# mLSTM heads: the mask of the first diagonal block moved to GpSimd, in place, ahead of a batch's finishing steps

## What is computed

```
log_fg = where(lower triangle, cum[s] - cum[t], -inf)
log_D  = log_fg + ig[t]
max_log_D = max(log_D, axis=-1)
D  = exp(log_D - max_log_D)
C  = (q k^T / sqrt(32)) * D
Cn = C / (max(|sum C|, exp(-max_log_D)) + 1e-6)
h  = Cn v
mu = mean(h);  var = mean((h - mu)^2)
out = (h - mu) * rsqrt(var + 1e-6) * ln_scale
x   = x + out
```

## Time and profile before

| what | value |
|---|---|
| median of three runs | 1442.99 us (1439.77 to 1443.45) |
| profiled execution, its own time | 1437.92 us |
| its span (first to last instruction) | 1436.1 us |
| mean granted TensorE clock | 0.896 |
| busy: PE / DVE / ACT / POOL | 78% / 61% / 35% / 32% |
| head stage, from the first load's landing to the last GpSimd instruction | 512.8 to 710.1 us |

### The profile page before, as it was taken

The page is one execution under the profiler, slowest core; times in us unless marked ns, Lnnn a source line. Parts: engine busy times, 40 slices in busy tenths (PEclk is TensorE's granted clock), DMA queues, the critical chain, the costliest instruction groups (busy, mean ns, idle before and its releaser), DMA issues. The chain is left out here.

```text
span 1436.1 us, 22899 instructions
## 1 busy us (share of the span) xinstructions
PE 1126.7 (78%) x6304; PEld 855.0 (60%) x6322; DVE 870.6 (61%) x1590; ACT 495.8 (35%) x1051; POOL 455.5 (32%) x344
## 2 busy tenths in 40 slices
PE   7998898788848468898178881559999999999942
PEld 6988665344425258787166650447777776777730
DVE  3344478788746348877254438945767767666515
ACT  2231252666622256775021110013333333333310
POOL 0000011111000005866722210125566656566520
PEclk9999899999989769887679995869999999999985
DMA  6210500000016495660131007058789988877639
GB/s 238 72 66 3 187 1 1 1 0 0 1 35 224 144 264 160 188 190 1 52 123 39 29 15 249 0 175 183 201 189 232 239 205 232 200 193 187 119 48 362
DMA packets 117608, 181.20 MB, mean 126 GB/s; under 512 B 13401, under 2 KB 48729, under 8 KB 117568
## 3 DMA queue, kind: packets, MB, share of 16 engines
q1 hardware_dynamic: 97184, 137.40, 29.6%
q0 software_dynamic: 18080, 38.85, 13.9%
q10 hardware_dynamic: 2304, 4.46, 0.8%
HBM read 138.76 MB, written 46.93 MB: 129 GB/s over the span
## 5 line engine op out<-in xcount | busy, mean ns | idle before, releaser
L2001 POOL DMA_INDIRECT y_d<-x_eo,x_ox x80 | 168.6, 2107 | 136.3 <-ACT x_eo L2157 113.5
L204 POOL TENSOR_TENSOR ln_rstd<-ln_ve,powers 128x2 f32<-128x2 f32 (+1 forms) x40 | 25.5, 638 | 326.0 <-DVE ln_ve L198 326.0
L2060 PE MATMUL x_h<-x_w_hi,x_t_hi 128*128 x320 | 127.4, 398 | 1.8 <-DVE x_t_lo L2173 1.8
L2062 PE MATMUL x_h<-x_w_hi,x_t_lo 128*128 x320 | 127.1, 397 | 0.0
L2061 PE MATMUL x_h<-x_w_lo,x_t_hi 128*128 x320 | 127.1, 397 | 0.0
L2173 DVE TENSOR_TENSOR x_w_lo<-w,x_w_hi (+1 forms) x64 | 109.4, 1750 | 0.0
L1988 POOL DMA_INDIRECT x_g<-r_d,x_ix x82 | 87.5, 1067 | 65.6 <-issue 46.9
L2133 ACT ACTIVATE x_gs<-x_h 128x256 f32<-128x256 f32 x80 | 30.6, 383 | 189.7 <-PE x_h L2062 179.6
L2173 DVE TENSOR_TENSOR x_t_lo<-x_xb,x_t_hi 128x512 fp32r<-128x512 f32 x80 | 55.3, 691 | 52.5 <-ACT x_t_hi L2128 52.5
L1412 DVE SCALAR_TENSOR_TENSOR h_c<-h_qk,h_d 128x768 f32<-128x768 f32 x64 | 58.1, 948 | 31.4 <-PE h_qk L1361 27.9
L1312 ACT ACTIVATE h_d<-h_negm,h_g 128x256 f32<-128x256 f32 x128 | 63.7, 498 | 36.4 <-DVE h_negm L1401 35.1
(11 more groups left out here) (343 smaller groups left out, 2786.1 us busy)
## 6 DMA issues: line engine op xcount, KB each, us to landing
w<-in_L_ffn_w SPq DMA_DIRECT2D x32, 1024.0 KB, 7.9
h_negm<-negm_d SPq DMA_DIRECT2D x16, 1024.0 KB, 9.2
w<-in_L_ffn_w SPq DMA_DIRECT2D x32, 512.0 KB, 9.9
raw<-in_L_ffn_w SPq DMA_DIRECT2D x3, 2816.0 KB, 15.7
x_res<-in_x SPq DMA_DIRECT2D x8, 512.0 KB, 4.8
ctx_in<-in_ctx SPq DMA_DIRECT2D x8, 512.0 KB, 4.0
m_cx<-in_ctx SPq DMA_DIRECT2D x8, 512.0 KB, 4.0
qt_d<-m_qt SPq DMA_DIRECT2D x8, 512.0 KB, 4.6
```

The source lines that it names most:

```text
L2001: nc.gpsimd.indirect_dma_start(out=y_d[s], out_offset=bass.IndirectOffsetOnAxis(ap=ox[q][:, s:s + 1], axis=0), in_=eo[q][s][:], in_offset= ...
L2060: nc.tensor.matmul(hbank[s][:], hi[:, k, :], w13p[0][:, at, k, :], start=k == 0, stop=False)
L2062: last = nc.tensor.matmul(hbank[s][:], lo[:, k, :], w13p[0][:, at, k, :], start=False, stop=k == KD - 1)
```

## The change

GpSimd adds the mask to slot 0 in place, 512 columns a group, and counts it on a semaphore of its own (`masked_near`). DVE's `mask` keeps slot 2 alone, also 512 columns. ScalarE's `decays` waits for both. GpSimd's program becomes a sequence of batches like the others': mask(b,2), centre(b-1), mask(b,3), mask(b+1,0), mask(b+1,1), finish(b-1).

```
         def mask(m, k, u):
+            near = nm[:, u, HG * k:HG * (k + 1), 0, :]
+            pool.wait_ge(ld[u], LOADS * m + LOADS)
+            nc.gpsimd.tensor_tensor(near, near, future[:].unsqueeze(1).to_broadcast([P, HG, P]),
+                                    ALU.add).then_inc(masked_near, 1)
+        def batch(b, m, u, first=False, final=False):
+            mask(m, 2, u)
+            if not first:
+                centre(b - 1, 1 - u)
+            mask(m, 3, u)
+            if not final:
+                mask(m + u, 0, 1 - u)
+                mask(m + u, 1, 1 - u)
+            if not first:
+                finish(b - 1, 1 - u)
...
-            with steps.loop(0, B // 2, 6) as i:
-                for u in range(2):
-                    centre(2 * i + u, u)
-                    finish(2 * i + u, u)
+            mask(0, 0, 0)
+            mask(0, 1, 0)
+            batches(lambda lo, hi: steps.loop(lo, hi, 6), lambda *v: batch(*v, first=True), batch,
+                    lambda *v: batch(*v, final=True))
+            centre(B - 1, 1)
+            finish(B - 1, 1)
...
                 act.wait_ge(masked, n + 1)
+                act.wait_ge(masked_near, n + 1)
...
-                nc.vector.tensor_tensor(nm[:, u, heads, 0::2, :], nm[:, u, heads, 0:2, :],
-                                        future[:].unsqueeze(1).unsqueeze(1).to_broadcast([P, HG, 2, P]),
-                                        ALU.add).then_inc(masked, 1)
+                nc.vector.tensor_tensor(nm[:, u, heads, 2, :], nm[:, u, heads, 1, :],
+                                        future[:].unsqueeze(1).to_broadcast([P, HG, P]), ALU.add).then_inc(masked, 1)
```

More of the change, by code:

```diff
@@ L1207, in mlstm @@
         (fills, dve_step, g_staged, v_staged, masked, d_ready, qk_ps, c_ready, pv_ps, h_sb, h_read, hc_in, hc_ready,
-         sq_ready, var_ready, rs_ready, pool_step, x_added) = (
+         sq_ready, var_ready, rs_ready, pool_step, x_added, masked_near) = (
             sem("h_" + n) for n in ("fills", "dve_step", "g_staged", "v_staged", "masked", "d_ready", "qk_ps",
                                     "c_ready", "pv_ps", "h_sb", "h_read", "hc_in", "hc_ready", "sq_ready",
-                                    "var_ready", "rs_ready", "pool_step", "x_added"))
+                                    "var_ready", "rs_ready", "pool_step", "x_added", "masked_near"))
         block = sh.enter_context(nc.Block())
@@ L1285, in finish, with mask @@
                 nc.gpsimd.tensor_tensor(x[:, ds(CB * b, CB), :], x[:, ds(CB * b, CB), :], flat, ALU.add).then_inc(x_added, 1)
+            def mask(m, k, u):
+                near = nm[:, u, HG * k:HG * (k + 1), 0, :]
[12 more added lines that the diff above has]
+                    finish(b - 1, 1 - u)
             for opened in (hc_ready, rs_ready, x_added):
                 pool.sem_inc(opened, OPEN)
-            with steps.loop(0, B // 2, 6) as i:
-                for u in range(2):
-                    centre(2 * i + u, u)
-                    finish(2 * i + u, u)
+            mask(0, 0, 0)
[4 more added lines that the diff above has]
+            finish(B - 1, 1)
         @block.scalar
```

## The result

The changed kernel takes 1460.41 us in the median of four runs (1457.19 to 1461.62), against 1442.38 for the kernel before: a ratio of 1.0124, 95% interval 1.0103 to 1.0146. It is slower by 18.0 us. The forecast was 1454.5, with a range of 1445.5 to 1463.0: the sign and the range hold, and the size was forecast at 11.5 us.

The account below looks back on a forecast made before the run. No engine was full in the head stage, bound by a ring of waits. Five new rings of 23.4 us, a last of 22 (+11.0) and a start 0.5 later gave +11.5 on 1442.99: 1454.5 us, range 1445.5 to 1463.

Parts of the forecast that it names:

- The mechanism: Head stage: decays(b,2) waits for GpSimd's mask(b,2), directly behind finish(b-2), closing a ring over one batch of 23.4 us.
- GpSimd's mask: Each of GpSimd's four masks of 512 columns a batch was taken at 1.27 us.
- DVE's half: DVE's mask, halved to 512 columns, goes from 1.21 to 0.691 us, four times a batch.
- The rival of the dear mask: GpSimd's mask costs 1.91 us, so a ring grows by 1.9 us: 1466 us in all; chance 0.07.
- The undisturbed ring: One batch's ring in the head stage: 21.5 us with nothing held up, 23.4 taken with port holds, 24.4 at most.
- covered by 2.6 us: PE's values(b,1) at the low clock end 2.6 us before ACT's take(b,1), so the clock costs nothing.
- the sum: Five rings of 23.4 us and a last of 22 make 139.0 against 128.04, +11.0; with the start, +11.5 us.
- The start: The first finishing comes about 0.5 us later, since DVE's and GpSimd's masks go one after the other.
- Nothing ties these two: In the kernel before, ACT's decays(2,2) starts 6.9 us before GpSimd's finish(0) ends, and neither depends on the other.
- On the path ... 1.04 us: The two DVE masks around the division lie on the path; halving them saves 1.04 us a batch.
- the faster rival: GpSimd's masks come in time, so DVE's gain in six batches gives -6.2 us: 1436.8 us; chance 0.04.
- The power instruction that holds DVE: Rival: DVE's mask and division wait for GpSimd's power instruction, ring about 1 us longer, 24.4, 1460.5 us; chance 0.02.

Follow-up runs that it names:

- e2: The changed kernel with GpSimd's four masks run in a tile of their own, ACT not waiting, first diagonal block left unmasked: 1434.00 us, ratio 0.9931.
- e4: The changed kernel with all four GpSimd masks of the next batch placed between centre(b-1) and finish(b-1): 1442.25 us, ratio 1.0001.
- e5: The changed kernel with GpSimd's masks of groups 0 and 1 of the next batch put behind the finishing: 1528.42 us, ratio 1.0599.
- e10b: The changed kernel with the mean's scaling by 1/32 (L1429) moved from DVE to GpSimd: 1453.31 us, ratio 1.0068.
- e3: The changed kernel with the mask of group 2 also put ahead, so only group 3's stays behind the earlier finishing: 1446.15 us, ratio 1.0024.
- e1: The kernel before with DVE masking only the second diagonal block and nobody masking the first: 1434.43 us, ratio 0.9938.
- e6: The kernel before with GpSimd masking the first diagonal block of groups 2 and 3 only, a batch ahead: 1443.52 us, ratio 1.0014.

## Why the prediction was right, and where it was not

- **The mechanism** (decays(b,2) behind finish(b-2), a ring over one batch) is shown: by ACT's waits of 7.8 and 8.6 us right in front of decays(b,2), by e2 and e4, where the same work without the wait costs next to nothing (stages of 196.4 and 199.0 us against 197.2), and by e5, where a longer ring costs 86 us over before.
- **GpSimd's mask** was taken at 1.27 us, and its median is 1.27 (1.26 to 2.25). DVE's half was taken at 0.69: 0.68 when nothing holds it, but 1.18 in the median of its 32, so that DVE's busy time in the stage fell by 5.3 us and not by 17. The rival of the dear mask, 1.91, falls.
- **The undisturbed ring** was taken at 23.4: the four rings of after without a long division are 22.5, 23.4, 23.2 and the last, 21.5 for the 22 forecast; in e10b 23.6. Inside, the multiplications took 2.95 (3.23 forecast), the scaling 2.5 to 2.8 (2.15 to 2.8), and the mask at the addition's end 1.72 (1.96). The lower end, 21.5 with nothing held, did not come.
- **The step that failed** is "covered by 2.6 us, so the clock ... costs none in the new ring". It was worked out from a weigh(b,1) that ends 1.3 us before mask(b,2) starts. I had DVE's holds lengthen GpSimd's instructions, and did not ask what GpSimd's do to the division. In the first ring weigh(2,1) ended 1.8 us after mask(2,2) started (568.28 against 566.48). In two of six rings the division's multiplication was held for 1.7 us, PE idled for 5.7 and 5.1 us in place of 3, and its low clock lasted into scores(b,3). The two rings measured 25.5 and 28.5: 7.2 us over the sum's 46.8, more than the 5.6 us by which the six rings miss the forecast (144.6 against 139.0). Two of before's rings already ran so, at the low level into scores(b,3) (22.8 and 22.9 us); the forecast read one ring, 20.45 us long, and the mean of all six. A held division is not enough by itself: in e3, e4 and e10b the first one is held as long, and the ring is 23.6 to 23.9.
- **The start** was forecast 0.5 us later; the first addition came 51.3 us after the landing in place of 53.6, 2.3 us earlier. The tail is 15.4 us, as forecast. The stage adds up: 16.6 - 2.3 - 0.2 = 14.1. That it lies only 2.6 us over the forecast is in part luck: the rings cost 5.6 us more than the sum and the start 2.8 less, and in e3, e4 and e10b the first addition comes 53.4 us after the landing again, so I have no cause for the early start. The profiled executions are 19.1 us apart, 5 of them outside the stage, for which the sum had no term; the medians are 18.0 apart, and the range held with 2.6 us to spare.
- **Nothing ties these two** was said of ACT's decays(2,2) and finish(0), and that holds; but the text saw the hold at GpSimd's scaling in the earlier trace rows and did not ask what it ties: DVE's division to the finishing of the batch before. DVE's gain "On the path ... 1.04 us", and with it the price of -6.2 for the faster rival, rested on that: e1's first two rings and e6 show 0 for it, e1's whole stage 3.5 us.
- **A reading** of the rows was 0.1 us off, without weight in the sum: the addition ends at 566.47, not at "566.35 or so", so DVE's mask(2,3) ended 1.1 us after it and `centre` 1.8 us after that mask.
- **The power instruction that holds DVE** falls, as forecast: DVE's mask at 557.82 and the division's small steps at 560.15 run at their free length under it (555.73 to 561.16).

## What to carry to other kernels

Before work is given to an idle engine, write down its program in order and look at what stands in front of the new instruction: here the same four masks cost 0, 18 or 86 us by their place in the queue, and the busy share of the engine (32%) told nothing of it. A mask that depends only on a load belongs in front of the long sequence of the batch before, and all of them, not three of four (e4's stage is 4.2 us shorter than e3's); even then it gained nothing here (ratio 1.0001). When a ring is priced, follow both engines at a shared port, since an instruction of 0.2 us may stand in for a semaphore, and read TensorE's granted clock ring by ring, since a mean over rings hides which of them it makes long.

## What was not expected of the hardware

- A DVE instruction on 32 columns (L1429, 0.18 us when free) waits for the end of GpSimd's scaling beside it (L1284, 1024 columns): 0.43 to 1.34 us in seven of eight batches. Moving this one instruction gave 12 us, 0.87% of the kernel; how much of it the hold alone cost is not shown.
- The same matmuls, scores(b,2) and values(b,1), took 4.57 us at a granted clock of 1.00, 6.19 at 0.72 and 7.82 at 0.50. A DVE that let PE start 0.75 us earlier won nothing in that ring, since PE then ran at the low level from its first matmul.
- Who comes first is decided within 0.02 us (561.33 against 561.35), and DVE's 1.22 us become 2.97. The Trainium skill (SBUF — State Buffer, section Who interferes with whom) says the same, that issue order decides who blocks; it also says that the pair is held for the whole instruction. The trace agrees for instructions of 512 and 1024 columns and not for the power instruction on 32: DVE ran under its 5.42 us unhindered, in both kernels.
